# Last layer's expert blocks: 64 of the 192 channels in rounded parts, behind both fp32 products

## The reference

```python
# x: 4 images of 16x16 positions, 192 channels: 1024 tokens
x = x + conv_moe(group_norm(x))        # 8 experts, inner 512, top 2, and a shared expert
t = t + attention(layer_norm(t))       # 12 heads of 16, two softmaxes, a mask in between
h = layer_norm(t)
# last layer: 16 experts of inner width 384, top 2 of 16, and a shared expert
logits = h @ w_gate + expert_bias
topk_p, topk_i = top_k(softmax(logits), 2); topk_p /= sum(topk_p)
for e in range(16):
    routed += comb[:, e:e+1] * ((silu(h @ wg[e]) * (h @ wu[e])) @ wd[e])
t = t + shared + routed
```

## Time and profile before

| | us |
|---|---|
| time, median of 3 runs | 463.34 (462.84 to 464.28) |
| the profiled execution | 467.23 |
| its span, first to last instruction | 465.4 |
| TensorE busy in the span | 425.2 (91%) |
| VectorE busy | 225.7 (48%) |
| ScalarE busy | 158.6 (34%) |
| first product of the last layer (L1250), busy | 85.3 |
| second products of both layers (L1265), busy | 70.1 |
| mean granted clock of TensorE, as a share of the full one | 0.989 |

### The profile page before, as it was taken

The page is one execution under the profiler, slowest core; times in us unless marked ns, Lnnn a source line. Parts: engine busy times, 40 slices in busy tenths (PEclk is TensorE's granted clock), DMA queues, the critical chain, the costliest instruction groups (busy, mean ns, idle before and its releaser), DMA issues.

```text
span 465.4 us, 7581 instructions
## 1 busy us (share of the span) xinstructions
PE 425.2 (91%) x2303; PEld 303.3 (65%) x2304; DVE 225.7 (48%) x611; ACT 158.6 (34%) x399; POOL 125.3 (27%) x136
## 2 busy tenths in 40 slices
PE   0999989999999899988888779998999999999995
PEld 0755356666667888766676547555777777777784
DVE  3536342222222576889889764462533333333333
ACT  1033141222221145988778733211221212221210
POOL 3201044545554000000000000011354444554430
PEclk9999999999999999999999998799999999999999
DMA  8999001111100792000000697600110011100006
GB/s 229 274 311 295 20 24 45 37 38 40 42 23 1 210 355 107 1 0 2 2 1 0 161 241 191 190 10 3 32 34 27 23 29 37 38 28 14 0 0 203
DMA packets 18056, 38.62 MB, mean 83 GB/s; under 512 B 4420, under 2 KB 13892, under 8 KB 17586
## 3 DMA queue, kind: packets, MB, share of 16 engines
q1 hardware_dynamic: 9570, 29.66, 22.6%
q0 software_dynamic: 5280, 6.32, 4.8%
q10 hardware_dynamic: 3184, 2.36, 1.6%
HBM read 35.16 MB, written 7.67 MB: 92 GB/s over the span
## 4 chain that ended last, share of the span: by engine, by line
PE 83%; ACT 6%; DMA 5%; DVE 3%; issue 2%; ACTq 0%; DVEq 0%; SPq 0%; POOLq 0%
PE bank L1250 17%; PE bank L1265 14%; PE bank L1183 12%; PE bank L1244 8%; PE bank L1434 5%; PE bank L1257 4%; PE bank L1388 4%; DMA w_first<-y_rows 3%; PE bank L1450 3%; PE bank L1226 2%; PE bank L1169 2%; PE bank L1482 2%; ACT scratch L691 2%; ACT g_sh L691 2%; ACT xn_t L691 2%
## 5 line engine op out<-in xcount | busy, mean ns | idle before, releaser
L1250 PE MATMUL bank<-w_first,rows_t 96*128 x248 | 85.3, 487 | 0.2 <-issue 0.2
L521 POOL DMA_INDIRECT rows<-xn_rows,slot_tok x56 | 57.3, 1024 | 94.1 <-DVE slot_tok L871 32.5
L529 POOL DMA_INDIRECT y_rows<-y,slot_row x54 | 55.3, 1024 | 98.9 <-DVE y L939 58.3
L1265 PE MATMUL bank<-w_second,hid_t 128*128 x370 | 70.1, 329 | 4.6 <-DVE hid_t L924 2.8
L1265 PEld LDWEIGHTS bank<-w_second,hid_t 128*128 128x128 f32 x370 | 58.7, 190 | 7.1 <-issue 7.0
L1250 PEld LDWEIGHTS bank<-w_first,rows_t 96*128 96x128 f32 x248 | 44.7, 190 | 25.2 <-issue 0.4
L929 DVE TENSOR_TENSOR act_h<-bank,act_g 128x384 f32<-128x384 f32 x31 | 17.3, 558 | 59.1 <-PE bank L1250 59.1
L1244 PE MATMUL bank<-w_first,rows_t 96*128 (+1 forms) x92 | 43.5, 594 | 1.1 <-issue 1.0
L625 ACT ACTIVATE act_g<-bank 128x384 f32<-128x384 f32 x31 | 15.2, 491 | 72.2 <-PE bank L1250 72.2
L941 DVE TENSOR_TENSOR y<-bank,w_second 128x192 f32<-128x192 f32 x23 | 8.2, 358 | 63.7 <-PE bank L1265 63.7
L567 POOL COPY act_h<-o_inv 128x256 f32<-128x256 f32 x12 | 4.8, 402 | 122.3 <-DVE o_inv L1070 122.3
(11 more groups left out here) (181 smaller groups left out, 645.8 us busy)
## 6 DMA issues: line engine op xcount, KB each, us to landing
w_first<-in_gate_up SPq DMA_DIRECT2D x16, 576.0 KB, 9.4
w_second<-in_down SPq DMA_DIRECT2D x1, 4608.0 KB, 19.0
w_first<-in_fc SPq DMA_DIRECT2D x1, 3072.0 KB
w_second<-in_fc SPq DMA_DIRECT2D x1, 3072.0 KB, 28.5
rows<-xn_rows,slot_tok POOLq DMA_INDIRECT x56, 2.6
y_rows<-y,slot_row POOLq DMA_INDIRECT x54, 2.3
w_first<-in_x_t SPq DMA_DIRECT2D x2, 384.0 KB, 4.8
w_first<-in_w SPq DMA_DIRECT2D x1, 768.0 KB, 7.0
```

The lines of the kernel that those rows point to most:

```text
L521: pool.indirect_dma_start(rows[b % 2][:], None, xn_rows[L.l], bass.IndirectOffsetOnAxis(slot_tok[:, b:b + 1].bitcast(U32), 0), bounds_chec ...
L529: pool.indirect_dma_start(y_rows[L.l], bass.IndirectOffsetOnAxis(slot_row[:, b:b + 1].bitcast(U32), 0), y[b % 2][:], None, bounds_check=TO ...
L1250: ins = pe.matmul(bank[:, 5 + g, 0:I1], rows_t[0:CH, k, :], w(CH, (k * 2 + g) * I1, I1), start=(k == 0), stop=(k == NCH - 1))
L1265: ins = pe.matmul(bank[:, 1, 0:C], hid_t[:, tile(ic)], w(P, ic * C, C), start=(ic == 0), stop=(ic == L.IC - 1))
```

## The change

The 192 channels are cut into 128 and 64 instead of 96 and 96. The first 128 stay in fp32. The other 64 are held twice on the partitions: in HBM a row of `xn_rows[1]` is 256 wide, 192 channels and the last 64 again, so the second transpose gives the 64 channels in partitions 0 to 63 and once more in 64 to 127. Against it stands a buffer of weights per block: the high part of the 64 rows in partitions 0 to 63 (ScalarE), the low part in 64 to 127 (VectorE). One fp32r product of the rounded rows with it gives high x high + high x low; a second one, of the rows' low part (with zeros below), gives low x high. For gate and up together: two fp32 products, then four fp32r products.

```diff
 def rows_transpose(L, b, u, n):
     pe.wait_ge(L.rows_in[u], (n + 1) * 16)
+    n = P if L.l else CH
     for k in range(NCH):
-        ins = pe.transpose(bank[0:CH, 0, tile(k)], rows[u][:, k * CH:(k + 1) * CH], ident)
+        ins = pe.transpose(bank[0:n, 0, tile(k)], rows[u][:, k * n:(k + 1) * n], ident)
...
 def first(L, b, w, u):            # the last layer's part
+    for g in range(2):
+        pe.matmul(bank[:, 5 + g, 0:I1], rows_t1, w(P, g * I1, I1), start=True, stop=False)
+    pe.wait_ge(L.part_low, b + 1)
+    pe.wait_ge(L.rows_low_ready, b + 1)
     for g, done in enumerate((L.first_ps, L.up_ps)):
-        for k in range(NCH):
-            ins = pe.matmul(bank[:, 5 + g, 0:I1], rows_t[0:CH, k, :], w(CH, (k * 2 + g) * I1, I1),
-                            start=(k == 0), stop=(k == NCH - 1))
-        ins.then_inc(done, 1)
+        part = w_parts1[u][:, g * I1:(g + 1) * I1]
+        pe.matmul(bank[:, 5 + g, 0:I1], rows_high, part, start=False, stop=False)
+        pe.matmul(bank[:, 5 + g, 0:I1], rows_low[:], part, start=False, stop=True).then_inc(done, 1)
...
 def act_rows(act, L, b):
     act.wait_ge(L.rows_t_ps, b + 1)
+    if L.l:
+        nc.scalar.copy(rows_t1, bank[:, 0, 0:P])
+        nc.scalar.copy(rows_high, bank[:, 0, P:2 * P]).then_inc(L.rows_t_ready, 1)
+        return
...
+def act_part(act, L, b, u):
+    start = act.value_load(blk_weights[0:1, 0, bass.ds(b, 1)], min_val=0, max_val=(L.E - 1) * per_expert)
+    if not isinstance(b, int) or b >= 2:
+        act.wait_ge(L.up_ps, b - 1)
+    nc.scalar.copy(w_parts1[u][0:REST], rest_of(start)).then_inc(L.part_high, 1)
+# ScalarE's turn: act_block(b); act_rows(b + 1); act_part(b + 2, 1 - u)
...
+def part_low(L, b, u, start):
+    dve.wait_ge(L.part_high, b + 1)
+    v.tensor_tensor(w_parts1[u][REST:], rest_of(start), w_parts1[u][0:REST].bitcast(F32), ALU.subtract
+                    ).then_inc(L.part_low, 1)
+def rows_low_part(L, b):
+    dve.wait_ge(L.rows_t_ready, b + 1)
+    v.tensor_tensor(rows_low[0:REST], bank[0:REST, 0, P:2 * P], rows_high[0:REST].bitcast(F32), ALU.subtract
+                    ).then_inc(L.rows_low_ready, 1)
+def block_last(L, b, u, turn):
+    at = part_at(L, b + 1)        # a register load
+    hid_copy(L, b - 1)
+    part_low(L, b + 1, u, at)
+    product(L, b)
+    rows_low_part(L, b + 1)
+    result(L, b - 1, u, turn)
+# blocks_last: parts of blocks 0 and 1, product(0); block_last(1); diag0; block_last(2); diag1;
+# then two blocks a turn of the loop, from block 3
...
+def load_expert(eng, e):
+    eng.dma_start(gate_up[:, e, 0], d["gate_up"][:, e]).then_inc(s_w1a, 16)             # 128 rows
+    eng.dma_start(gate_up[0:REST, e, 1], d["gate_up_rest"][:, e]).then_inc(s_w1a, 16)   # 64 rows
+def store_rows(eng):
+    eng.dma_start(by_tile(xn_rows[1])[:, :, 0:C], xn_tok[:]).then_inc(xn_stored, 16)
+    eng.dma_start(by_tile(xn_rows[1])[:, :, C:], xn_tok[:, :, P:]).then_inc(xn_stored, 16)
...
-rows = [sb(f"rows{i}", [P, C]) for i in range(2)]
+rows = [sb(f"rows{i}", [P, 2 * P]) for i in range(2)]
```

More of the change, by code:

```diff
@@ L625, in act_block, with rest_of, act_blocks_last, act_blocks @@
                 nc.scalar.activation(act_g[:], bank[:, 5, 0:I1], ACT.Silu).then_inc(L.gate_act, 1)
-        def act_blocks(act, L):
-            if L.l:
-                act_rows(act, L, 0)
+        def rest_of(start):
+            return w_first[0:REST, 2 * I1:][:, 0:(E1 - 1) * per_expert + 2 * I1][:, bass.ds(start, 2 * I1)]
+        def act_part(act, L, b, u):
[3 more added lines that the diff above has]
+            nc.scalar.copy(w_parts1[u][0:REST], rest_of(start)).then_inc(L.part_high, 1)
+        def act_blocks_last(act, L):
+            act.wait_ge(L.expert_ready, len(L.sizes))
+            act.wait_ge(s_w1a, 32 * E1)
+            act.wait_ge(L.slots_ps, 1)
+            act_part(act, L, 0, 0)
+            act_rows(act, L, 0)
+            act.wait_ge(L.sh_c_ps, 2 * L.IC)
+            act_part(act, L, 1, 1)
             act_block(act, L, 0)
             act_rows(act, L, 1)
-            if L.l == 0:
-                act.wait_ge(s_qkvw, 32)
-                nc.scalar.copy(w_high, wqkv).then_inc(w_high_ready, 1)
+            act_part(act, L, 2, 0)
+            with act.Fori(0, (L.NB - 3) // 2) as i:
+                for u in range(2):
+                    b = i * 2 + (u + 1)
+                    act_block(act, L, b)
+                    act_rows(act, L, b + 1)
+                    act_part(act, L, b + 2, 1 - u)
+            for b in (L.NB - 2, L.NB - 1):
+                act_block(act, L, b)
+                act_rows(act, L, b + 1)
+        def act_blocks(act, L):
+            act_block(act, L, 0)
+            act_rows(act, L, 1)
+            act.wait_ge(s_qkvw, 32)
+            nc.scalar.copy(w_high, wqkv).then_inc(w_high_ready, 1)
             with act.Fori(0, (L.NB - 1) // 2) as i:
@@ new lines, in blocks_last @@
+            def blocks_last(L):
+                dve.wait_ge(L.expert_ready, len(L.sizes))
+                dve.wait_ge(s_w1a, 32 * E1)
+                part_low(L, 0, 0, part_at(L, 0))
+                rows_low_part(L, 0)
+                part_low(L, 1, 1, part_at(L, 1))
+                product(L, 0)
+                rows_low_part(L, 1)
+                block_last(L, 1, 0, 0)
+                route(L, "diag0")
+                block_last(L, 2, 1, 0)
+                route(L, "diag1")
+                with dve.Fori(0, (L.NB - 5) // 2) as i:
+                    for u in range(2):
+                        block_last(L, i * 2 + (u + 3), u, i + 1)
+                block_last(L, L.NB - 2, 0, (L.NB - 3) // 2)
+                b = L.NB - 1
+                hid_copy(L, b - 1)
+                product(L, b)
+                result(L, b - 1, 1, (L.NB - 3) // 2)
+                hid_copy(L, b)
+                result(L, b, 0, (L.NB - 1) // 2)
@@ L1108, in _ @@
                 stage(L1, s)
-            blocks(L1)
+            blocks_last(L1)
             for j in OWN[1]:
@@ L1287, in blocks @@
                 hid_transpose(L, 1)
-                first(L, 2, weights(L, 2, 0))
+                first(L, 2, weights(L, 2, 0), 0)
                 rows_transpose(L, 3, 1, 1)
```

75 lines of the change are left out of this document (39 added, 36 removed).

## The result

The changed kernel takes 451.16 us (median of 4 runs, 449.70 to 451.97) beside 463.81 for the kernel before on the same chip: ratio 0.973, 95% interval 0.970 to 0.975, 12.65 us less. Forecast were 15.2 less and 448.1, with 445.5 to 454.5 as the range.

A forecast was written before the change was run, and what follows sets the result against it. TensorE's instruction stream was taken as the bound. Gains of 0.88 up to block 4, 26 x (4.108 - 3.58) = 13.73 and 0.60 for block 30 sum to 15.2 us: 463.34 becomes 448.1, 8-in-10 range 445.5 to 454.5.

The forecast's parts named there:

- main term: TensorE's stream per block in the last layer's block phase: 3.51 us instead of 4.11, 0.60 less a block.
- The edits costed at nothing: Split weight loads, second row store, wider fill, extra GpSimd copy and first block's parts: all covered, no time added.
- The period: Time per block in the loop: 3.51 stream, 0.02 new TensorE waits, 0.05 VectorE lateness, 3.58 us; 4.108 before.
- the 3.7 that the prediction named as a sign of being wrong: Block period over 3.7 us, or TensorE waiting for rows or parts instead of VectorE's product, would show the prediction wrong.
- Rival A: VectorE bounds the block with the loop's turn, 0.4 to 0.6 late every second block: period 3.78, 453.3 us; 18%.
- C: Rival: gathers land late because landing grows with the row, 3.5 against 3.2 us of cover: period about 3.8, 454; 5%.
- the queue of GpSimd: Gather b+4 starts 2.36 into a block, lands 2.6 later; its cover before the row transpose shrinks from 1.7 to 0.6 us.
- VectorE behind the loop's turn: VectorE's product delays TensorE's hidden transpose by 0.10 us every second block (bounds 0 and 0.5), 0.05 on the mean.
- The slack of 0.11: Hidden transpose can start at 3.07 us into a block, TensorE wants it at 3.18: slack 0.11 us instead of 0.44.
- From block 0's start to block 4's: Start of the block phase: block 1 3.51, block 2 4.24, block 3 4.25 us; block 4 starts 0.88 earlier than before.
- Rival B: VectorE's subtraction with two SBUF inputs waits for GpSimd's descriptor work in each block: period 3.95, 457.7 us; 5%.
- The 2 us that it might have cost: VectorE's low part and following product held by the partition-group rule: turn's block about 0.16 later, time 2 us higher.

The follow-up runs named there:

- kernel before with wide rows: Kernel before with the last layer's rows 256 wide, a second store and gathers of 1024 B a row, products as before: 463.96 us beside 463.69, ratio 1.001.
- second profile: Profile of the changed kernel run once more, unedited: 451.47 us, ratio 0.972 of before; phase 115.55 us.
- first profile: Profile of the changed kernel's first measurement, 451.16 us, with one gather that took 5.1 us to land and block 4 at 5.86 us.
- the four moves: Changed kernel with gather ahead of scatter, TensorE's register load early, VectorE's behind the hidden copy, diagonal matrices one place earlier: 446.33 us, 0.961 of before; repeated 446.36.
- the gather first: Changed kernel with GpSimd issuing the gather of block b+4 ahead of the scatter of block b: 448.21 us, 0.964 of before.
- the four moves without low x high: The four moves, with two of the four fp32r products of each block left out: 439.43 us, 0.947 of before.
- VectorE's register load late: Changed kernel with VectorE reading the weights' start into a register behind the hidden copy instead of ahead of it: 451.57 us, 0.971 of before.

## Why the prediction was right, and what it missed

Right was the main term. TensorE's stream was forecast at 3.51 and is 3.51; an fp32r record of 384 columns at 0.173 and is 0.17, with rows of 512 and 192 columns alone to go by the earlier trace rows. Rounding 0.83 (0.82), row copies 0.27 (0.26), low part 0.95 (0.95), rows' low part 0.27 (0.29), SiLU 1.84 after the block's start (1.91), product done at 3.00 (3.01). The edits costed at nothing cost nothing that shows: block 0 starts at 316.4 us in the changed kernel and at 316.8 in the kernel before with wide rows, in profiles that are at the full clock throughout.

The period was mis-sized: 3.58 forecast, 3.67 measured (blocks 4 to 30 of the second profile in 95.40 us), and 26 x 0.09 = 2.3 are the 2.3 us by which its phase gained less than 15.2. The first profile, with the stall, had 3.74, which is over the 3.7 that the prediction named as a sign of being wrong. The measured time lies in the stated range because this was wide enough for rivals A and C; the way in which the time was lost is neither of them. The step that failed is the queue of GpSimd: "The cover shrinks from 1.7 to 0.6", taken as enough. The cover was 0.2 to 0.35 in the slowest blocks (gather 2.48 into the block instead of 2.36, which every second block of the kernel before has as well, 2.7 to landing instead of 2.6, wanted at 5.50 instead of 5.56), and, above all, it was counted up to the instruction that needs the rows, while a register load of 0.7 us (as long as VectorE's) stands behind that instruction's wait in TensorE's sequencer. The cover that is needed is 0.75 in a turn's first block. In those 26 periods 4.0 us lie above 3.514 each, the period with the four moves; 0.5 stay with the gather first and are VectorE's, 0.3 are block 4, where a lengthened gather landed late (below), the rest is this. "Wrong it would be ... with TensorE's waits for rows" came half true.

VectorE behind the loop's turn was forecast 0.10 late in every second block and is 0.05: the product starts 2.57 into block 7 (forecast 2.65). Rival A stays a rival with a price of 0.6 us. The slack of 0.11 is about right: with 0.17 taken out of it the product is late by 0.09 in the even blocks of the four moves without low x high (3.26 against 3.17), so it was 0.08.

From block 0's start to block 4's it took 15.83 us in the first profile and 15.74 in the second, forecast 15.80, but by errors that cancel: block 1 took 4.0 instead of 3.51, since the register load for block 2 stands behind the hidden transposes' wait for VectorE (0.72 to the next first product, as in block 0; the same mechanism, read right for block 0 and overlooked for block 1), block 2 took 3.88 instead of 4.24. That this part of the sum came out is luck.

Rival B (the subtraction waits for GpSimd) fell with its sign turned. The subtraction was not lengthened in this kernel. GpSimd's operation was, when it began while VectorE's ran. Timelines of the changed kernel, start of the low part first:

```profile
326.09 0.95 DVE L1011 TENSOR_TENSOR w_parts_odd<-w_first,w_parts_odd 64x768 fp32r<-64x768 f32 x1
...
326.20 1.75 POOL L549 DMA_INDIRECT rows<-xn_rows,slot_tok  x1 [0.30 <-issue]
...
327.07 0.56 DVE L993 TENSOR_TENSOR act_h<-bank,act_g 128x384 f32<-128x384 f32 x1
...
327.55 0.27 DVE L1017 TENSOR_TENSOR rows_low<-bank,rows_high 64x128 fp32r<-64x128 f32 x1
```

In the traces, gathers and scatters that began 0.05, 0.10, 0.32, 0.52, 0.71 and 0.80 us behind the start of a subtraction of 0.95 took 1.81, 1.73, 1.52, 1.33, 1.13 and 1.05 us instead of 1.02: the end is 1.83 to 1.86 behind the subtraction's start in these, and 1.82 to 1.87 in all 93 such pairs of the traces. In the changed kernel 4 of 63 (one of them behind the diagonal matrices, one ahead of the first block) took 1.13 to 1.75; in the loop GpSimd mostly starts first (342.74 against 342.91), and both keep their length. The price shows in block 4 of the second profile: its gather took 1.52, landed 3.3 us after its start, and the block took 3.85, where it is 3.51 when no parts are made.

The Trainium skill, page "SBUF — State Buffer", section "Who interferes with whom", says that the order of issue decides who blocks; these rows agree where VectorE is first by 0.05 us or more, and show no block of VectorE where GpSimd is first. With VectorE first by 0.01 to 0.03 (13 times with VectorE's register load late, 12 times with the four moves) it is the other way: GpSimd keeps 1.02 to 1.03 and the subtraction takes 1.00 to 1.01.

The rule of the Trainium skill, page "VectorE: DVE Perf Modes", section "Two Vector instructions with no wait between them", shows in the same rows: the low part ends at 327.04 and the product starts at 327.07, while the rows' low part starts 0.08 before the product's end. That is 0.11 us for the pair. The 2 us that it might have cost in the turn's blocks did not come; the chain ahead of it was shorter than forecast: the hidden copy starts 1.00 into block 7 (346.10) instead of 1.17.

## What to carry to other kernels

When blocks get shorter, every lead that was counted in time shrinks with them, and it must be measured up to the last thing that stands behind the wait in the same sequencer, a register load above all, not up to the instruction that uses the data. "Issue" in front of TensorE with no engine named is worth a look at its sequencer's rows. And two remedies whose gains together exceed the loss have one cause in common, as a saving on the bounding engine that brings nothing points to a queue beside it. A load moved ahead of a wait is not gone: when the blocks became shorter still, it held the transposes itself.

## What the runs showed of the hardware

- A TensorE register load from SBUF takes 0.7 us of its sequencer (a load of 0.30 to 0.36 and register steps around it), and nothing behind it is issued meanwhile; from the landing of the rows to the second product it is 0.97 us with a wait in front.
- An indirect gather or scatter of GpSimd that started 0.05 to 0.80 us behind the start of VectorE's subtraction with two SBUF inputs (0.95 us) ended 1.82 to 1.87 us behind that start (93 cases in eleven traces), so it took up to 1.81 us instead of 1.02, the subtraction none longer. With 0.01 to 0.03 us between the starts the subtraction took 1.00 to 1.01.
- fp32r products of 384 columns in the same accumulation as fp32 ones start 0.17 us apart and cost nothing at the switch: the block's stream is the sum, 3.51.
